# Normalised rows of the second routing made on ScalarE with a scale and a shift, instead of on GpSimd, in an attention and mixture-of-experts kernel

## The chip, the cores and the metric

The kernel runs on one core of a Trainium2 chip. Five engines work side by side, each through its own list of instructions in order: TensorE (PE in the profile, with its weight loads as PEld), VectorE (DVE), ScalarE (ACT), GpSimd (POOL) and SyncE (SP, which only issues transfers). An engine waits for another by semaphores. The metric is the device time of one execution in microseconds (us), lower is better.

## The reference

The input x has 8 batches of 256 tokens of 128 numbers, all float32. Three blocks follow each other, each adding to x:

```
x = x + 0.5 * ffn(layernorm(x))     # block f1
x = x + attn(layernorm(x))          # block at
x = x + 0.5 * ffn(layernorm(x))     # block f2
```

`layernorm(x)` is `(x - mean) / sqrt(var + 1e-5)` over the 128 numbers of a token. `ffn` is a mixture of 8 experts: a router (`xt @ Wr + br`) picks 2 experts for each token, each expert is two matrix products with a relu and a layernorm behind each, and the two results are weighed and added. `attn` is differential attention with 8 heads: two softmax maps for each head, one subtracted from the other, then a division by the root of the mean square of each head (rms) and an output projection.

## The kernel before

The order of the instructions is written out by hand; no planner is involved. The three blocks overlap. The middle of the program is a loop of *turns*, t = 2 to 9, in which each engine does pieces of four stages for four different batches:

- stage A, batch t (turns 2 to 7): layernorm, projections, packing of q and k;
- stage B, batch t-1 (to turn 8): scores for the row maxima (`scores(n)` on PE, six pieces; `row_max(b, n)` on DVE, line 2134);
- stage C, batch t-2: transposed scores (`scores_t(g)`, g = 0 to 7, on PE, lines 1900 to 1908), the exponential of each (`expo(g)` on ACT, line 1712), and products with the values (lines 1918 to 1922);
- stage D, batch t-3: combination of the maps (`outputs`, DVE line 2165), squares (`squares`, ACT line 1696), mean squares (DVE lines 2170 and 2171), the power -1/2 of them on POOL (line 1658, tile `orr`), its use on DVE (`rms`, line 2180), output projection, residual.

In turns 4 to 9 the *second routing*, for block f2, is worked in, for batch d = t-4: `row_stats` on DVE writes means and variances of the two tiles of 128 tokens into `mv`; `batch_norm(d)` on POOL (lines 1614 to 1623) makes the reciprocal deviation `rstd` (a power -1/2, line 1619) and then the normalised rows, one instruction of 128x128 for each tile (line 1622), into `rows_of` (the trace names it row_buf). Each of these adds 1 to the semaphore `F["xn"]` (f2_xn in the lists of order). Four things wait for it: `turn_batch(d)` on PE (line 627), which transposes the two tiles, `second_copies` on SP, which copies the rows once more beside themselves, the indirect transfers on POOL that scatter the rows to memory (line 459), and, for the last two batches, nothing of this change (`late_norm` on DVE makes their rows).

What matters is where these stand in the lists of the engines. ACT in a turn goes: expo(0), expo(1), copy of the transposed attention rows (line 917), `turned_batch` (line 620, copies the result of `turn_batch`), `squares`, expo(2), a copy of q (line 937), expo(3), and so on; in turn 9 `squares` stands between expo(0) and expo(1). PE goes: scores_t(0), scores(0), scores_t(1), transposes of the attention rows (line 1170, turns to 7), `turn_batch`, scores_t(2), scores(1), a projection (line 1176), scores_t(3), the router's products (`batch_logits`, lines 636 and 638), scores(2), and so on. While stage B runs, scores_t(g) may start only when expo(g-1) is done, since one pair of PSUM banks holds them, and scores(n) only when row_max(n-1) is done. POOL goes: power for the attention layernorm (line 559), `batch_norm`, then gathers or scatters of rows, `combine` (lines 1599 to 1605, turns to 6), and the power for the rms (line 1658).

Of the kernel before, what the change touches and what calls it, by code (L numbers as in the profile page):

```python
# [17 lines left out]
ALU = mybir.AluOpType  # L18
ACT = mybir.ActivationFunctionType
# [3 lines left out]
BATCH, SEQ, DIM = 8, 256, 128  # L23
# [26 lines left out]
HALF = TT // 2  # L50
# [58 lines left out]
def build(nc, x, Wq, Wk, Wv, Wo, lq1, lk1, lq2, lk2, Wr, br, W1, b1, g1, be1, W2, b2, g2, be2, out, stages=("f1", "at", "f2")):  # L109
    with ExitStack() as ctx:  # L110
        def sb(name, shape, dt=F32):
            return ctx.enter_context(nc.sbuf_tensor(name, shape, dt))
# [15 lines left out]
        xs = sb("xs", [P, TT, DIM])  # L128
        row_buf = [sb(f"row_buf{i}", [P, HALF * TOPK * ROW]) for i in range(2)]
        xn = row_buf[0][:, 0:TT * DIM].rearrange("p (t d) -> p t d", d=DIM)  # L130
# [25 lines left out]
        rows_of = [v[:].rearrange("p (t k w) -> p t k w", k=TOPK, w=ROW) for v in row_buf]  # L156
# [16 lines left out]
        mv = sb("mv", [P, TT, 2])  # L173
        sdev = sb("sdev", [P, TT])
        rstd = sb("rstd", [P, TT])
# [4 lines left out]
        m12 = sb("m12", [P, TOPK, TT])  # L180
# [1097 lines left out]

        def late_norm(dve, S, step, d):
            a, b = 2 * d, 2 * d + 2  # L1280
            dve.wait_ge(S["sd"], 2 * (BATCH - 2) + d - 5)
            step(dve.reciprocal(rstd[:, a:b], sdev[:, a:b]))
            for t in range(a, b):
                dve.tensor_scalar(rows_of[1][:, t % HALF, :, 0:DIM], xs[:, t, None, :].to_broadcast([P, TOPK, DIM]), mv[:, t, 0:1],
                                  rstd[:, t:t + 1], ALU.subtract, ALU.mult).then_inc(S["xn"], 1)
# [292 lines left out]
        def att_gpsimd(pool, S):  # L1578
# [33 lines left out]
            F = sems["f2"]  # L1612

            def batch_norm(d):
                a, b = 2 * d, 2 * d + 2
                pool.wait_ge(F["mv"], b)
                pool.tensor_scalar(sdev[:, a:b], mv[:, a:b, 1], EPS, None, ALU.add).then_inc(F["sd"], 1)
                pool.wait_ge(F["sd"], b - 1)
                pool.tensor_tensor(rstd[:, a:b], sdev[:, a:b], neg_half[:, 0:2], ALU.pow).then_inc(F["sd"], 1)
                pool.wait_ge(F["sd"], b)  # L1620
                for t in range(a, b):
                    pool.tensor_scalar(rows_of[t // HALF][:, t % HALF, 0, 0:DIM], xs[:, t, :], mv[:, t, 0:1], rstd[:, t:t + 1],
                                       ALU.subtract, ALU.mult).then_inc(F["xn"], 1)

            pool.wait_ge(S["yst0"], 8 * PAIRS)
            pool.wait_ge(S["yst1"], 8 * PAIRS)
# [50 lines left out]
        def att_scalar(act):  # L1677
# [7 lines left out]
            F = sems["f2"]  # L1685
            copy_xT, relu, copy_hT, sqrt1, sqrt2, finish = scalar_pair(act, F, False)

            def half_values(s, seq):

                act.wait_ge(A["o"], seq * 2 + s + 1)  # L1690
                act.copy(oTs[:, s].rearrange("p a e -> p (a e)"), bank[s][:]).then_inc(A["oTv"], 1)

            def squares(d):

                act.wait_ge(A["dstep"], d * D_STEPS + 3)
                act.activation(osq, od[:], ACT.Square).then_inc(A["dstep"], 1)
# [6 lines left out]
            def turn(t, par):  # L1703
                A_, B_, C_, D_ = stages_of(t)
                b, c, d = t - 1, t - 2, t - 3

                def expo(g):
                    act.wait_ge(A["st"], c * 8 + g + 1)
                    if not (isinstance(c, int) and c == 0):
                        act.wait_ge(A["o"], c * 2 - 1 + g // 4)  # L1710
                    low = 0 if B_ or g % 2 == 0 else 2
                    act.activation(prob[:, g], quad[:, low:low + 2, 0:3 * P], ACT.Exp).then_inc(A["prob"], 1)  # L1712
# [10 lines left out]
                if C_:  # L1723
                    expo(0)
                    if t == BATCH + 1:
                        squares(d)
                    expo(1)
                if A_:
                    turned_norm(act, t, bank[7])
                if 4 <= t <= BATCH + 1:  # L1730
# [32 lines left out]
            d = BATCH - 1  # L1763
# [618 lines left out]

        b1s = early[0:32, 5760:5760 + P]
        pads = sb("pads", [P, 8])
        hold, spad, gpad = pads[0:1, 0:2], pads[:, 2:3], pads[0:1, 4:6]


# [144 lines left out]
```

## Time and profile before

| what | value |
|---|---|
| time, median of 3 runs | 447.54 us (446.53 to 448.34) |
| span of the profiled execution, first to last instruction | 444.6 us |
| the profiled execution's own time | not recorded apart from its span |
| PE, DVE, ACT, POOL busy | 395.1, 348.4, 286.7, 246.8 us |
| turns 4 to 9 | about 207 to 320 us of the span |
| PE clock granted in the turns | full (1.00 in each stretch) |

The busy share says little about who holds up whom, since each engine's list is fixed and the turns run from one engine to another and back. A start time in a timeline, with the idle time and the releaser in brackets behind it, tells who was late. Times below are microseconds from the span's start.

### The profile page before, as it was taken

The page shows a single profiled execution, that of the slowest core. Times are in us where ns is not written, and L with a number is a line of the kernel's source. Part 1 is how long each engine was busy: PE and PEld are TensorE (multiplying, and loading weights), DVE is VectorE, ACT ScalarE, POOL GpSimd, SP SyncE. Part 2 cuts the span into 40 slices and gives each one's busy share as a digit, 9 for nine tenths or more (in the row PEclk, how much of TensorE's full clock was granted, in tenths as well). Part 3 has the DMA queues.
Part 4 walks back from the last instruction along what each step waited for, and adds up shares of the span by engine and source line. Part 5 has one row for each costly group of instructions (what it writes and reads, how often), then busy time and mean ns, then how long its engine had stood idle before and what let it go on. Part 6 is the DMA issues. An engine that isn't in the chain of part 4 may idle for free.

```text
span 444.6 us, 11683 instructions
## 1 busy us (share of the span) xinstructions
PE 395.1 (89%) x3605; PEld 278.5 (63%) x3606; DVE 348.4 (78%) x1302; ACT 286.7 (64%) x589; POOL 246.8 (56%) x348
## 2 busy tenths in 40 slices
PE   7989999999898857889888889976899899999984
PEld 7735487877676744556564656554577677878733
DVE  5886578887959886878897988976688968788865
ACT  1395687755676754787677777764765467667630
POOL 8685554436461136374847566576634758555540
PEclk9996999999999955999999999999999899999999
DMA  7920114554443411000000001001121221111127
GB/s 219 335 96 14 35 49 143 181 178 158 121 144 112 170 37 35 21 8 20 25 13 25 24 21 33 25 27 36 56 60 34 72 64 56 53 59 47 37 72 244
DMA packets 25862, 35.17 MB, mean 79 GB/s; under 512 B 4282, under 2 KB 18546, under 8 KB 24659
## 3 DMA queue, kind: packets, MB, share of 16 engines
q1 hardware_dynamic: 20866, 24.62, 16.7%
q0 software_dynamic: 4944, 9.90, 7.6%
q8 instruction: 28, 0.46, 0.4%
q14 instruction: 24, 0.19, 0.1%
HBM read 15.45 MB, written 18.24 MB: 76 GB/s over the span
## 4 chain that ended last, share of the span: by engine, by line
PE 51%; DVE 20%; issue 9%; POOL 8%; ACT 5%; DMA 3%; DVEq 1%; SPq 1%; POOLq 0%; ACTq 0%
PE bank L972 11%; PE bank L991 10%; PE bank L981 5%; DVE mx L2134 4%; POOL xr_scratch L459 3%; PE bank L1181 3%; PE bank L2495 2%; PE bank L1900 2%; DMA early<-y_scratch 2%; PE bank L1176 2%; ACT early L1712 1%; PE bank L1918 1%; POOL orr L1658 1%; PE bank L1852 1%; DMA y_scratch<-yo,dest_u 1%
## 5 line engine op out<-in xcount | busy, mean ns | idle before, releaser
L991 PEld LDWEIGHTS bank<-w2c,hT 128*128 128x128 f32 x624 | 76.5, 194 | 23.5 <-issue 22.6
L991 PE MATMUL bank<-w2c,hT 128*128 x624 | 78.1, 279 | 4.9 <-ACT hT L760 4.9
L972 PE MATMUL bank<-w1s,xT 128*128 x156 | 74.1, 596 | 0.7 <-DVE w2c L2369 0.6
L2134 DVE TENSOR_REDUCE mx<-bank 128x4 f32<-128x1024 f32 (+1 forms) x48 | 58.5, 1220 | 13.7 <-PE bank L1861 13.3
L1712 ACT ACTIVATE early<-bank 128x768 f32<-128x768 f32 x64 | 51.8, 812 | 23.7 <-PE bank L1908 23.0
L1377 DVE BATCH_NORM_STATS2 st<-wide 128x6 f32<-128x512 f32 x78 | 50.1, 683 | 19.8 <-ACT wide L754 19.7
L760 ACT COPY hT<-bank 128x1024 f32<-128x1024 f32 (+1 forms) x40 | 39.5, 988 | 34.0 <-PE bank L981 34.0
L513 POOL DMA_INDIRECT xgw<-xn_scratch,slot_u x39 | 37.4, 960 | 35.4 <-PE bank L961 24.3
L483 POOL DMA_INDIRECT y_scratch<-yo,dest_u x39 | 39.0, 1001 | 31.3 <-PE bank L981 16.8
L579 POOL DMA_INDIRECT yk<-y_scratch,posi x32 | 32.2, 1005 | 42.2 <-DMA y_scratch<-yo 17.4
L754 ACT ACTIVATE wide<-bank 128x1024 f32<-128x1024 f32 (+1 forms) x40 | 40.0, 1001 | 10.3 <-PE bank L972 9.6
L459 POOL DMA_INDIRECT xr_scratch<-row_buf,hi_i x32 | 31.8, 994 | 22.6 <-PE bank L1908 12.9
L981 PE MATMUL bank<-ident,wide 128*128 128x128 f32 x312 | 40.9, 274 | 1.3 <-issue 1.3
L972 PEld LDWEIGHTS bank<-w1s,xT 128*128 128x128 f32 x156 | 27.0, 190 | 22.0 <-issue 21.6
L981 PEld LDWEIGHTS bank<-ident,wide 128*128 128x128 f32 x312 | 35.3, 142 | 2.6 <-issue 2.0
L937 ACT COPY wide<-bank 128x1024 bf16<-128x1024 bf16 x28 | 28.4, 1014 | 5.7 <-PE bank L1181 5.6
L775 ACT ACTIVATE yo<-yz,r 128x128 f32<-128x128 f32 x78 | 27.1, 396 | 4.2 <-DVE yz L1420 2.6
L1396 DVE SCALAR_TENSOR_TENSOR yy<-bank,r,b2p 128x128 f32<-128x128 f32 x78 | 24.6, 351 | 6.1 <-DVE r L1390 1.6
L1900 PE MATMUL bank<-mxT,sel 64*128 64x384 bf16 x128 | 22.2, 343 | 7.2 <-ACT early L1712 5.1
L1852 PE MATMUL bank<-mrhs,mlhs 64*128 64x128 bf16 (+1 forms) x192 | 16.1, 248 | 11.4 <-DVE mx L2134 6.6
L1420 DVE SCALAR_TENSOR_TENSOR yz<-yy,mv,g2b 128x128 f32<-128x128 f32 x78 | 23.3, 339 | 0.0
L559 POOL TENSOR_TENSOR ars<-ave,neg_half 128x2 f32<-128x2 f32 x8 | 5.8, 720 | 31.2 <-DVE ave L2092 31.2
(380 smaller groups left out, 893.4 us busy)
## 6 DMA issues: line engine op xcount, KB each, us to landing
xr_scratch<-row_buf SPq DMA_DIRECT2D x8, 1032.0 KB
xgw<-xr_scratch SPq DMA_DIRECT2D x39, 64.5 KB, 1.8
y_scratch<-yo SPq DMA_DIRECT2D x19, 128.0 KB, 1.8
w1s<-in_L_ffn_W_dram SPq DMA_DIRECT2D x1, 2048.0 KB, 9.9
early<-y_scratch SPq DMA_DIRECT2D x8, 256.0 KB, 3.4
xn_scratch<-row_buf SPq DMA_DIRECT2D x1, 1024.0 KB
out_dram<-xs SPq DMA_DIRECT2D x8, 128.0 KB, 2.6
row_buf<-row_buf SPq DMA_DIRECT2D x6, 128.0 KB
```

The lines of the kernel that those rows point to most:

```text
L459: pool.indirect_dma_start(out=xr_dram, out_offset=bass.IndirectOffsetOnAxis(ap=slot2[:, c:c + 1], axis=0), in_=rows_of[t // HALF][:, t % H ...
L483: pool.indirect_dma_start(out=y_dram, out_offset=bass.IndirectOffsetOnAxis(ap=dest_u[:, 2 * p + j:2 * p + j + 1], axis=0), in_=yo[:, p % 2 ...
L513: pool.indirect_dma_start(out=xg[:, u, :], out_offset=None, in_=xn_dram, in_offset=bass.IndirectOffsetOnAxis(ap=slot_u[:, n:n + 1], axis=0 ...
L579: pool.indirect_dma_start(out=yk4[:, t % (2 * YRING), k, :], out_offset=None, in_=done, in_offset=bass.IndirectOffsetOnAxis(ap=posi[:, c:c ...
L754: act.activation(hh[:, u, 0:k, :], banks[:, h_at[u]:h_at[u] + k, :], ACT.Relu).then_inc(S["relu"], 1)
L760: act.copy(hT[:, u, 0:k, :], banks[:, 5:5 + k, :]).then_inc(S["hTc"], 1)
L972: last = pe.matmul(bank[h_at[u] + j][:], xT[:, u, j, :], w1s[:, bass.ds(e * FF, FF)], start=True, stop=True)
L981: last = pe.transpose(bank[5 + j][:, c * P:c * P + P], hh[:, u, j, c * P:(c + 1) * P], ident[:])
L991: last = pe.matmul(o[:, j * DIM:(j + 1) * DIM], hT[:, u, j, c * P:(c + 1) * P], w2c[:, bass.ds(e * (FC * DIM) + c * DIM, DIM)], start=(c = ...
L1377: last = dve.bn_stats(st1[:, u, j, :], hh[:, u, j, :])
L1712: act.activation(prob[:, g], quad[:, low:low + 2, 0:3 * P], ACT.Exp).then_inc(A["prob"], 1)
L2134: dve.tensor_reduce(mx[:, c:c + 2 * per].rearrange("p (a q) -> p q a", q=2), quad[:, low:low + 2, :].rearrange("p q (a e) -> p q a e", a=p ...
```

## The change

`batch_norm` on POOL no longer writes the rows. It makes four small tiles of 128x2 instead of two: the variance plus eps, minus the mean (new), the power -1/2, and the shift, minus mean times `rstd` (new). A new function `batch_rows(d)` on ACT then makes the two 128x128 tiles as `Identity(x * rstd + shift)`, with the scale and the shift read from tiles, one number for each partition. It stands in turns 4 to 9 right behind expo(1). Semaphore counts follow. The tiles `mean_at` and `shift_at` are parts of `m12`, which is free by then.

```diff
         def late_norm(dve, S, step, d):
             a, b = 2 * d, 2 * d + 2
-            dve.wait_ge(S["sd"], 2 * (BATCH - 2) + d - 5)
+            dve.wait_ge(S["sd"], 4 * (BATCH - 2) + d - 5)
...
                 pool.tensor_scalar(sdev[:, a:b], mv[:, a:b, 1], EPS, None, ALU.add).then_inc(F["sd"], 1)
-                pool.wait_ge(F["sd"], b - 1)
+                pool.tensor_scalar(mean_at[:], mv[:, a:b, 0], -1.0, None, ALU.mult).then_inc(F["sd"], 1)
+                pool.wait_ge(F["sd"], 4 * d + 2)
                 pool.tensor_tensor(rstd[:, a:b], sdev[:, a:b], neg_half[:, 0:2], ALU.pow).then_inc(F["sd"], 1)
-                pool.wait_ge(F["sd"], b)
-                for t in range(a, b):
-                    pool.tensor_scalar(rows_of[t // HALF][:, t % HALF, 0, 0:DIM], xs[:, t, :], mv[:, t, 0:1], rstd[:, t:t + 1],
-                                       ALU.subtract, ALU.mult).then_inc(F["xn"], 1)
+                pool.wait_ge(F["sd"], 4 * d + 3)
+                if d:
+                    pool.wait_ge(F["xn"], 2 * d)
+                pool.tensor_tensor(shift_at[:], mean_at[:], rstd[:, a:b], ALU.mult).then_inc(F["sd"], 1)
...
+            def batch_rows(d):
+
+                act.wait_ge(F["sd"], 4 * d + 4)
+                for t in range(2 * d, 2 * d + 2):
+                    act.activation(rows_of[t // HALF][:, t % HALF, 0, 0:DIM], xs[:, t, :], ACT.Identity, scale=rstd[:, t:t + 1],
+                                   bias=shift_at[:, t % 2:t % 2 + 1]).then_inc(F["xn"], 1)
+
...
                     expo(1)
+                if 4 <= t <= BATCH + 1:
+                    batch_rows(t - 4)
                 if A_:
                     turned_norm(act, t, bank[7])
...
+        mean_at, shift_at = m12[:, 0, 0:2], m12[:, 1, 0:2]
```

ACT in turn 7 (d = 3), from the second copy of k to expo(2), before:

```order
L937 COPY wide<-bank 128x8x128 [waits at_kTp]
L1712 ACTIVATE early<-bank 128x768 [waits at_o,at_st] x2
L917 COPY axT<-bank 128x256 [waits at_xTp]
L620 COPY xnT<-bank 128x256 [waits f2_lgp,f2_xnTp]
L1696 ACTIVATE turned_o<-od 128x256 [waits at_dstep]
L1712 ACTIVATE early<-bank 128x768 [waits at_o,at_st]
```

and the same place now (line numbers behind the new function are 8 higher; m is the tile m12):

```order
L937 COPY wide<-bank 128x8x128 [waits at_kTp]
L1720 ACTIVATE early<-bank 128x768 [waits at_o,at_st] x2
L1698 ACTIVATE row_buf<-xs,m,rstd 128x128 [waits f2_sd]
L1698 ACTIVATE row_buf<-xs,m,rstd 128x128
L917 COPY axT<-bank 128x256 [waits at_xTp]
L620 COPY xnT<-bank 128x256 [waits f2_lgp,f2_xnTp]
L1704 ACTIVATE turned_o<-od 128x256 [waits at_dstep]
L1720 ACTIVATE early<-bank 128x768 [waits at_o,at_st]
```

Two instructions stand new between expo(1) and the copies; nothing else of ACT's order moved.

POOL in turn 7, from the attention's power to the power for the rms, before:

```order
L559 TENSOR_TENSOR ars<-ave,neg_half 128x2 [waits at_var]
L1617 TENSOR_SCALAR sdev<-mv 128x2 [waits f2_mv]
L1619 TENSOR_TENSOR rstd<-sdev,neg_half 128x2 [waits f2_sd]
L1622 TENSOR_SCALAR row_buf<-xs,mv,rstd 128x128 [waits f2_sd]
L1622 TENSOR_SCALAR row_buf<-xs,mv,rstd 128x128
L459 DMA xr_scratch<-row_buf,hi_i 17280x129 [waits at_st,f2_xn,f2_pos]
L459 DMA xr_scratch<-row_buf,hi_i 17280x129 [waits f1_xnst,at_st]
L1658 TENSOR_TENSOR orr<-oms,neg_half 128x16 [waits at_msq]
```

and now:

```order
L559 TENSOR_TENSOR ars<-ave,neg_half 128x2 [waits at_var]
L1617 TENSOR_SCALAR sdev<-mv 128x2 [waits f2_mv]
L1618 TENSOR_SCALAR m<-mv 128x2
L1620 TENSOR_TENSOR rstd<-sdev,neg_half 128x2 [waits f2_sd]
L1624 TENSOR_TENSOR m<-m,rstd 128x2 [waits f2_xn,f2_sd]
L459 DMA xr_scratch<-row_buf,hi_i 17280x129 [waits at_st,f2_xn,f2_pos]
L459 DMA xr_scratch<-row_buf,hi_i 17280x129 [waits f1_xnst,at_st]
L1659 TENSOR_TENSOR orr<-oms,neg_half 128x16 [waits at_msq]
```

Two large instructions are gone and two small ones are there. The order of PE, DVE and SP is the same as before.

## Rows read from the trace of the kernel before

**Rows 1.** Waits, 185 to 330 us: who waited for whom, total, times, longest (us).

```profile
PEld bank L1900 <- ACT early L1712: 11.7, 24, 1.5
```

**Rows 2.** Instructions by line, POOL, 190 to 330 us: busy us, mean ns.

```profile
L1622 POOL TENSOR_SCALAR row_buf<-xs,mv,rstd 128x128 f32<-128x128 f32 x12 | 10.1, 842 | 0.7
L1617 POOL TENSOR_SCALAR sdev<-mv 128x2 f32<-128x2 f32 x6 | 1.5, 242 | 2.9 <-DVE mv L1190 2.8
```

**Rows 3.** Instructions by line and form, ACT, whole span.

```profile
L775 ACT ACTIVATE yo<-yz,r 128x128 f32<-128x128 f32 x78 | 27.1, 396 | 4.2 <-DVE yz L1420 2.6 <-DMA y_scratch<-yo,dest_u 1.4
L768 ACT ACTIVATE sd<-mv,eps_c 128x2 f32<-128x2 f32 x38 | 11.0, 289 | 6.7 <-DVE mv L1408 6.6
L923 ACT COPY vnew<-bank 128x128 f32<-128x128 f32 x16 | 4.4, 274 | 0.0
L812 ACT ACTIVATE pads<-eps_c 128x1 f32<-128x1 f32 x1 | 0.2, 203 | 0.0
```

**Rows 4.** Timeline of ACT, 333 to 339 us: start, length, instruction.

```profile
335.52 0.68 ACT L775 ACTIVATE yo<-yz,r 128x128 f32<-128x128 f32 x2
```

**Rows 5.** Timelines of turn 7 (268.8 to 288.1 us): ACT, PE, DVE.

```profile
273.76 0.81 ACT L1712 ACTIVATE early<-bank 128x768 f32<-128x768 f32 x1 [0.71 <-PE bank L1908]
...
274.72 0.39 ACT L620 COPY xnT<-bank 128x256 f32<-128x256 f32 x1
...
275.30 0.82 ACT L1712 ACTIVATE early<-bank 128x768 f32<-128x768 f32 x1
...
274.19 0.41 PE L627 MATMUL bank<-ident,row_buf 128*128 128x128 f32 x2
274.63 0.34 PE L1900 MATMUL bank<-mxT,sel 64*128 64x384 bf16 x2
...
278.22 1.23 DVE L2134 TENSOR_REDUCE mx<-bank 128x4 f32<-128x1024 f32 x1 [0.20 <-PE bank L1861]
```

**Rows 6.** Timelines of turn 8 (288.1 to 306 us): PE, DVE.

```profile
293.49 0.42 DVE L2165 TENSOR_TENSOR od<-ow 128x256 f32<-128x256 f32 x1
...
293.93 0.34 PE L1900 MATMUL bank<-mxT,sel 64*128 64x384 bf16 x2 [0.54 <-ACT early L1712]
...
294.93 0.17 DVE L2171 TENSOR_SCALAR oms<-oms 128x16 f32<-128x16 f32 x1
```

**Rows 7.** Timeline of turn 4 (207.4 to 228.0 us), all engines.

```profile
212.25 0.81 ACT L1712 ACTIVATE early<-bank 128x768 f32<-128x768 f32 x1 [0.71 <-PE bank L1908]
...
212.68 2.07 DVE L2165 TENSOR_TENSOR od<-ow 128x256 f32<-128x256 f32 x1
...
215.69 0.76 DVE L2171 TENSOR_SCALAR oms<-oms 128x16 f32<-128x16 f32 x1
...
216.36 1.21 DVE L2134 TENSOR_REDUCE mx<-bank 128x8 f32<-128x1024 f32 x1
```

**Rows 8.** Timeline of turn 5 (228.0 to 248.7 us), all engines.

```profile
237.63 2.94 POOL L1658 TENSOR_TENSOR orr<-oms,neg_half 128x16 f32<-128x16 f32 x1
...
240.60 0.42 DVE L2180 TENSOR_TENSOR od<-od,orr 128x256 f32<-128x256 f32 x1 [1.44 <-POOL orr L1658]
```

**Rows 9.** Timelines of turn 6 (248.7 to 268.8 us): DVE, ACT.

```profile
253.68 0.81 ACT L1712 ACTIVATE early<-bank 128x768 f32<-128x768 f32 x1 [0.71 <-PE bank L1908]
...
254.11 1.30 DVE L2165 TENSOR_TENSOR od<-ow 128x256 f32<-128x256 f32 x1
...
255.76 0.79 ACT L1712 ACTIVATE early<-bank 128x768 f32<-128x768 f32 x1
...
258.93 1.22 DVE L2134 TENSOR_REDUCE mx<-bank 128x4 f32<-128x1024 f32 x1 [0.54 <-PE bank L1861]
```

**Rows 10.** Timeline of turn 9 (306 to 320 us), all engines.

```profile
311.12 0.80 ACT L1712 ACTIVATE early<-bank 128x768 f32<-128x768 f32 x1
...
311.38 0.41 PE L627 MATMUL bank<-ident,row_buf 128*128 128x128 f32 x2 [0.87 <-POOL row_buf L1622]
...
316.84 0.42 DVE L2180 TENSOR_TENSOR od<-od,orr 128x256 f32<-128x256 f32 x1 [1.36 <-POOL orr L1658]
```

## The prediction, on record before the changed kernel ran

> **What bounds the kernel now.** I read the table of waits of the attention turns first, then the timelines of turns 4 to 9 engine by engine, then the instructions by line for prices. The change touches nothing outside these turns, so only they count. What the reader should see: TensorE and ScalarE pass the turn to and fro. the transposed scores waited 11.7 us in 24 places for the exponential before them [rows 1], and each exponential needs its scores. That is one loop, scores_t(g), expo(g), scores_t(g+1), and time put into it between expo(1) and scores_t(2) is not hidden by either engine's idle time. In turns 7 and 8 nothing else is late at that place: scores_t(2) starts at 274.63, 0.06 behind the end of expo(1) at 274.57 [rows 5], and at 293.93 with "<-ACT early" as its releaser [rows 6]. The transposes of the normalised rows (line 627) lie at 274.19, beside expo(1), where they cost nothing, because GpSimd had the rows ready before.
>
> GpSimd is the other candidate. In turn 5 VectorE waits 1.44 us for its power of the mean squares (tile orr), in turn 9 1.36 us, and in turn 9 TensorE waits 0.87 us for the rows themselves [rows 8, 10]. So a lighter GpSimd is worth something in two or three turns, and nothing in the others.
>
> **What is removed.** Twelve GpSimd instructions of 0.84 us, two in each of six turns [rows 2]. Added on GpSimd are two of 128x2 in each turn. Minus the mean is of the kind of line 1617, 0.24 us. The shift is a product of two 128x2 tiles, which the trace does not show at that size; I take the same 0.24, since the instruction is of the same size, with 0.1 for the semaphore between. So GpSimd is free 1.68 - 0.58 = 1.1 us earlier in each turn. Bounds: 1.68 if the small ones cost nothing, 0 if each took as long as a removed one. It finishes the shift well ahead of expo(1)'s end, so ScalarE does not wait for it: in turn 9, where it is latest, TensorE got the rows at 311.38 [rows 10], the shift would be there at about 310.2, and expo(1) ends at 311.92.
>
> **What is added on ScalarE.** Two instructions of 128x128 with scale and bias both read from tiles. The trace has none of these. The nearest is line 775, one operand from a tile, 0.396 us, and 0.68 for a pair [rows 3, 4]. A bias read from a tile costs 0.289 - 0.203 = 0.086 (line 768 against 812); the same step shows between line 923, 0.274, and line 775. So one takes about 0.48. The pair, with the overlap of 2 x 0.396 - 0.68 = 0.11 that line 775 shows, takes 0.85, and since it overlaps expo(1)'s end as well, it ends 0.75 behind it. Bounds: 0.34 (two like line 923, with both overlaps) and 0.96 (two of 0.48 end to end). The Trainium skill ("ScalarE: Activation LUTs", section "What ACT_TABLE_LOAD costs") gives 186 ns plus 0.833 ns for each element, 93 ns more for each pointer operand, and an overlap of 93; that makes 0.48 and 0.87 for the pair, beside line 775's 0.396 against the page's 0.386.
>
> **What it costs on the path.** `turn_batch` now waits for ScalarE, and behind it on TensorE stands scores_t(2). Behind expo(1)'s end come: 0.75 for the rows, 0.07 for the semaphore, 0.44 for the transposes (274.19 to 274.63 [rows 5]). scores_t(2) thus starts 1.26 behind expo(1) instead of 0.06: 1.2 us later. ScalarE's side is longer still: it waits for these transposes before its copy (line 620), and copy and squares take 0.58 (274.72 to 275.30 [rows 5]), so expo(2) cannot start before 2.0 us behind expo(1)'s end. What was 0.1 to 0.5 us of slack becomes the chain. Turn by turn:
>
> - Turn 7: expo(2) goes from 275.30 to 276.5, the products behind it and row_max(2) with them; row_max(2) waited for TensorE before (278.22 [rows 5]), so nothing absorbs it. +1.2.
> - Turn 8: the same loop, scores_t(2) at 293.93 [rows 6]. +1.2.
> - Turn 6: expo(1) ends at 254.49, expo(2) started 1.27 behind it, at 255.76, because DVE's `outputs` took 1.30 us where it took 0.42 in turn 8 [rows 6, 9]. It moves to 256.5, +0.7; row_max(2) at 258.93 is then held by TensorE's order about 0.5 later. +0.5.
> - Turn 4: `outputs` took 2.07 us, so squares and expo(2) were late anyway, and ScalarE's new path ends at 213.06 + 2.0 = 215.1, where expo(2) stood (212.68 + 2.07, then the squares). Then the small line 2171 took 0.76 at 215.69, against 0.17 in turn 8 [rows 6, 7]; this ought to shrink, since GpSimd will be past its adds. row_max(1) at 216.36 comes about 0.6 earlier. -0.6.
> - Turn 5: the +1.2 arrives at VectorE's `rms` at 240.4; the power, which started at 237.63 behind GpSimd's queue, starts 1.1 earlier at 236.5 and ends at 239.5. Before, `rms` was at 240.60 [rows 8]. -0.2.
> - Turn 9: expo(1) ends at 311.92, the transposes move from 311.38 to 312.75, the row of exponentials behind by 1.4. But `rms` waited for the power until 316.84 [rows 10] and TensorE behind it; that comes 1.1 earlier. What is left at the output projection is +0.3.
>
> Sum: 1.2 + 1.2 + 0.5 - 0.6 - 0.2 + 0.3 = +2.4 us. The span of 444.6 becomes 447.0. The runs' median lies 2.9 us above the span, which holds what is ahead of the first and behind the last instruction; I leave that as it is: 447.5 + 2.4 = 449.9.
>
> The contention in turns 4 and 6 is weighed once more, as it speaks for the change: `outputs` reads two SBUF tiles and took 2.07 and 1.30 us where GpSimd worked at the same time. The Trainium skill ("GPSIMD Engine Reference", "Specifications") says that GpSimd shares its SBUF interfaces with VectorE and contends with instructions of two SBUF inputs; the trace agrees with it by those two rows. By that the gain is in how GpSimd's work shifts against VectorE's, and 1.1 us of shift can take a hold away in one turn and make one in another (in turn 5, `outputs` starts where GpSimd's product then would). Both stand off ScalarE's new path of 2.0 us as long as the hold is under 1.5 us.
>
> **Rivals.** (a) *No measurable change.* The turns have more slack than I see: the delay of scores_t(2) is absorbed in row_max's own queue on VectorE, and only turns 7 and 8 pay, less the gains in 4, 5 and 9 (-0.6, -0.2, 0): 2.4 - 0.8 = +1.6; with the pair at its low bound, 0.34, the two turns pay 0.4 less each, +0.8. For it: VectorE is busy through most of a turn. Against it: in turn 7 row_max(2) still waited 0.20 for TensorE. Time 448.3 to 449.1. (b) *Faster.* GpSimd is the real bound: the two waits for the power (1.44, 1.36) and the wait for the rows (0.87) [rows 8, 10] go, 3.7 us at most, and turn 4's hold goes too (2.07 - 0.45 = 1.6). Turns 7 and 8 still pay 2.4, so 2.4 - 5.3 = -2.9, 444.6; it decides if the new step of 1.2 is hidden in turns 5, 6 and 9 altogether. Against it: ScalarE's chain of 2.0 us stands in all six turns. (c) *Every turn pays in full*: 6 x 1.2 = 7.2 us, 454.7, if the earlier GpSimd makes new holds on VectorE where it lifted old ones. (d) *Reload of ScalarE's table* for Identity between two exponentials would cost some 1.3 us twice in each turn, over 15 us; the order of the changed kernel has the same five loads as before, none in the turns, so I give it next to nothing.
>
> **How the numbers follow.** The forecast (+1.8 to +4) has 0.5, rival (a) 0.3 (+0.5 to +1.8), (b) 0.1 (below that), (c) and (d) 0.1. About 0.5%, 2.2 us, is what a measurement of this kernel can tell from no change, and the forecast lies just above that. Slower by over 0.5% (above 449.8): a little over half of the forecast's cases and all of (c), 0.47. Faster by over 0.5% (below 445.3): most of (b), 0.06. Within: 0.47. The range leaves out a part of (b) and of (c): 447.3 to 452.4. The forecast's own range is 449.3 to 451.5.
>
> **What would show it.** Right: line 1698 twice in each turn, 0.45 to 0.5 us each; the transposes at line 627 with ScalarE's rows as releaser in turns 5 to 9; scores_t(2) 1.2 to 1.3 behind expo(1)'s end; expo(2) 2.0 behind it; turns 7 and 8 1.2 us longer; orr about 1 us earlier against its turn in turns 5 and 9, and not the releaser of `rms` in turn 5. Wrong: turns 7 and 8 as long as before (19.3 and 17.9 us, by the stretches that head rows 5 and 6), or `rms` in turns 4 to 6 so early that the turns get shorter, or `outputs` held over 1.5 us in turns that had no hold.

## The result, and the profile after

| | before | after |
|---|---|---|
| time, median of 4 runs each | 447.24 us (446.53 to 448.34) | 456.54 us (456.28 to 457.72) |
| ratio, 95% interval | | 1.0195 [1.0153, 1.0237] |
| span of the profiled execution | 444.6 us | 455.8 us (its run: 457.72) |
| mean granted clock of TensorE | 0.965 | 0.949 |

Slower by 9.3 us (1.95%, clear of the noise), where +2.4 was forecast; the time lies 4 us above the range. First the page of the changed kernel: span, busy times, and the clock that TensorE was granted in 40 slices.

```profile
span 455.8 us, 11700 instructions
PE 401.2 (88%) x3605; PEld 281.2 (62%) x3606; DVE 347.8 (76%) x1302; ACT 291.8 (64%) x601; POOL 239.2 (52%) x348
PEclk9898999999999967999799999979799999999997
```

and the same line of the page of the kernel before:

```profile
PEclk9996999999999955999999999999999899999999
```

ScalarE got 5.1 us more work and GpSimd 7.6 less, as expected. But PE is busy 6.1 us longer with the same 3605 instructions, and its clock line shows a 7 in slices 20, 27 and 29 (of 11.4 us each, from 216.5, 296.2 and 319.0 us on), where the line of before has a 9 in all of them. (The low digits in slices 15 and 16 stand in both lines, ahead of the turns in question; the last slice, with a 7 for a 9, is behind them.) So there are two things to look for: the loop that the prediction spoke of, and TensorE's clock.

**The loop.** The waits from 185 to 340 us after (who waited for whom, total, times, longest), against [rows 1]:

```profile
ACT early L1720 <- PE bank L1918: 22.7, 27, 3.5
...
PE bank L627 <- ACT row_buf L1698: 9.6, 6, 2.3
DVE oms L2180 <- ACT turned_o L1704: 9.1, 7, 2.0
PEld bank L1910 <- ACT early L1720: 8.9, 19, 1.1
```

and the new instruction of ScalarE (ns min/median/max, first and last start):

```profile
L1698 ACT ACTIVATE row_buf<-xs,m,rstd x12: 482/482/491, 212.3 to 319.1; 128x128 f32<-128x128 f32 x12
```

In all six turns TensorE now waits for ScalarE's rows, which never happened before. Turn 7 of the changed kernel, PE and ACT, against [rows 5]:

```profile
275.88 0.81 ACT L1720 ACTIVATE early<-bank 128x768 f32<-128x768 f32 x1 [0.71 <-PE bank L1918]
276.59 0.87 ACT L1698 ACTIVATE row_buf<-xs,m,rstd 128x128 f32<-128x128 f32 x2
...
278.05 0.37 ACT L620 COPY xnT<-bank 128x256 f32<-128x256 f32 x1 [0.33 <-PE bank L627]
278.31 0.42 ACT L1704 ACTIVATE turned_o<-od 128x256 f32<-128x256 f32 x1
278.63 0.80 ACT L1720 ACTIVATE early<-bank 128x768 f32<-128x768 f32 x1
...
277.60 0.41 PE L627 MATMUL bank<-ident,row_buf 128*128 128x128 f32 x2 [1.39 <-ACT row_buf L1698]
277.94 0.34 PE L1910 MATMUL bank<-mxT,sel 64*128 64x384 bf16 x2
```

expo(1) ends at 276.69, scores_t(2) starts at 277.94, 1.25 behind it (forecast 1.26), and expo(2) at 278.63, 1.94 behind (forecast 2.0). The mechanism is there to the tenth.

**The clock.** I measure a turn from the first transposes of the row maxima (line 1931 before, 1941 after) to the next; turn 9 to the start of the step on VectorE that makes hi_i, the rows' places, for its batch (L699 after, the sixth of the second routing). In us:

| kernel | turn 4 | 5 | 6 | 7 | 8 | 9 to hi_i |
|---|---|---|---|---|---|---|
| before | 20.75 | 20.68 | 20.08 | 19.30 | 18.68 | 10.51 |
| changed | 23.30 | 20.52 | 20.49 | 20.48 | 22.27 | 12.18 |
| difference | +2.55 | -0.16 | +0.41 | +1.18 | +3.59 | +1.67 |
| forecast | -0.6 | -0.2 | +0.5 | +1.2 | +1.2 | +0.3 |

Turns 5, 6 and 7 came out within 0.1 of the forecast. Turns 4, 8 and 9 are 3.2, 2.4 and 1.4 longer than it, and these three hold the slices with a 7 in the clock line. Two stretches of turn 4, turn 8's and turn 9's in the changed kernel (length; busy us and instructions of PE, PEld, DVE, ACT, POOL; PEclk; DMA share, GB/s):

```profile
208.39:214.39 6.00, 4.09 (x67) 2.73 (x66) 4.22 (x7) 4.59 (x10) 5.11 (x12) 1.00 0.04 11
214.39:224.39 10.00, 10.00 (x111) 5.77 (x107) 6.14 (x15) 5.56 (x12) 4.55 (x3) 0.66 0.08 21
...
293.18:299.18 6.00, 3.72 (x65) 2.53 (x64) 2.84 (x5) 4.33 (x9) 3.31 (x5) 1.00 0.08 25
299.18:309.18 10.00, 8.84 (x115) 5.55 (x113) 5.95 (x13) 4.63 (x8) 5.01 (x3) 0.66 0.07 20
...
315.45:319.73 4.28, 1.39 (x26) 0.87 (x23) 3.09 (x12) 3.06 (x6) 2.77 (x5) 1.00 0.10 31
319.73:327.63 7.90, 7.90 (x78) 4.54 (x78) 4.40 (x27) 3.62 (x5) 3.35 (x2) 0.57 0.24 62
```

Each turn begins at 2.4 GHz (1.00); in the stretch that follows the wait for the rows most of the time is at 1.2 GHz, which I call half clock (from about 214.5 to 222, 300 to 307 and 320.5 to 327.5). The same products take up to 1.7 times as long there. Turn 8, PE:

```profile
298.08 0.41 PE L627 MATMUL bank<-ident,row_buf 128*128 128x128 f32 x2 [1.76 <-ACT row_buf L1698]
...
300.95 1.02 PE L638 MATMUL bank<-wrs,xnT 128*128 128x8 f32 x4
...
304.05 0.39 PE L1862 MATMUL bank<-mrhs,mlhs 64*128 64x128 bf16 x4 [0.47 <-DVE mx L2144]
...
304.80 1.08 PE L1928 MATMUL bank<-early,vaug 128*32 128x256 f32 x8
```

At full clock L638 takes 0.61 and L1928 0.64, as the runs below show. The rest of the +11.2 of the span: -0.7 ahead of turn 4, +1.4 from the sixth hi_i to the seventh, +1.2 in what follows, where either trace has half clock once more (352 to 356 before, 450 to the end after).

### The profile page after: what moved, and what is told of

Its sections match the earlier page's. It is cut to its first block, busy times and chain, and to the rows that moved or that the text cites. A ratio compares the mean times of both kernels' runs of the same rounds, so it can differ in the third digit from the quotient of the medians.

```text
span 455.8 us, 11700 instructions
## 1 busy us (share of the span) xinstructions
PE 401.2 (88%) x3605; PEld 281.2 (62%) x3606; DVE 347.8 (76%) x1302; ACT 291.8 (64%) x601; POOL 239.2 (52%) x348
## 4 chain that ended last, share of the span: by engine, by line
PE 54%; DVE 15%; issue 10%; ACT 8%; POOL 6%; DMA 5%; DVEq 1%; SPq 1%; POOLq 0%; ACTq 0%
PE bank L972 10%; PE bank L991 9%; PE bank L981 5%; DVE mx L2144 3%; PE bank L1181 3%; PE bank L1176 3%; ACT early L1720 3%; PE bank L1910 3%; POOL xr_scratch L459 2%; PE bank L1928 2%; DMA early<-y_scratch 2%; PE bank L1862 2%; PE bank L2361 1%; PE bank L1930 1%; PE bank L2011 1%
## 5 line engine op out<-in xcount | busy, mean ns | idle before, releaser
L991 PEld LDWEIGHTS bank<-w2c,hT 128*128 128x128 f32 x624 | 75.2, 192 | 24.3 <-issue 23.5
L991 PE MATMUL bank<-w2c,hT 128*128 x624 | 76.8, 276 | 5.7 <-ACT hT L760 5.7
L1659 POOL TENSOR_TENSOR orr<-oms,neg_half 128x16 f32<-128x16 f32 x7 | 20.5, 2932 | 5.2 <-DVE oms L2181 3.7
## 6 DMA issues: line engine op xcount, KB each, us to landing
w1s<-in_L_ffn_W_dram SPq DMA_DIRECT2D x1, 2048.0 KB, 10.9
```

The source lines that it names most:

```text
L991: last = pe.matmul(o[:, j * DIM:(j + 1) * DIM], hT[:, u, j, c * P:(c + 1) * P], w2c[:, bass.ds(e * (FC * DIM) + c * DIM, DIM)], start=(c = ...
```

## Experiments

All ratios are to runs of the kernel before on the same chip; edits are against the changed kernel. The median of the kernel before differs between these sets of runs, 447.15 to 448.32 us, so times of two experiments can be compared to about 1 us, and ratios are the better measure. A clock or a turn length is that of one traced execution. The turn lengths of all runs are in a table at the end of this section.

**rows_before_expo1**: the rows ahead of expo(1).

```diff
+                    if t in (4, 5, 6, 7, 8, 9):
+                        batch_rows(t - 4)
                     expo(1)
-                if 4 <= t <= BATCH + 1:
-                    batch_rows(t - 4)
```

> The changed kernel with the two row instructions on ScalarE between expo(0) and expo(1) (in turn 9 behind the squares) instead of behind expo(1). There ScalarE waited 0.71 us for TensorE before expo(1), the shift is ready (209.97 + 0.28 = 210.25 in turn 4, expo(0) ends at 210.86), and the rows are ready 0.8 us behind expo(0), before TensorE comes to the transposes. Theory 'wait on TensorE' (the loss is TensorE's wait for the rows and what follows from it): the wait of 1.39 to 2.32 us before line 627 goes, and with it the three stretches of half clock; GpSimd's 1.1 us stay saved: 445 to 447.5 us, against 456.5 for the change. Rival 'ScalarE's time' (0.87 us more in each turn on an engine in the loop is the loss wherever it stands): expo(1) and all behind it comes 0.8 later in each turn: 452 us or more.

446.21 us, ratio 0.9951 [0.9928, 0.9975]: half a per cent faster than the kernel before, and 10.3 us faster than the changed one. Its turn 7 (ACT and PE):

```profile
270.53 0.88 ACT L1698 ACTIVATE row_buf<-xs,m,rstd 128x128 f32<-128x128 f32 x2
271.34 0.81 ACT L1720 ACTIVATE early<-bank 128x768 f32<-128x768 f32 x1
...
271.56 0.41 PE L627 MATMUL bank<-ident,row_buf 128*128 128x128 f32 x2
272.20 0.34 PE L1910 MATMUL bank<-mxT,sel 64*128 64x384 bf16 x2 [0.24 <-ACT early L1720]
```

expo(1) waited 0.71 for its scores in turns 4 to 8; the pair takes up that idle time, and the transposes lie beside expo(1) again. Turns 7 and 8 are back at 19.29 and 18.67. So the place of the pair, not its work, costs the 1.2 us. The gain over before is in turns 4, 5, 6 and 9 (-0.75, -0.16, -0.79, -0.53: 2.2 together, which is the ratio's), where GpSimd was late. In this trace no turn runs at half clock.

**transpose_later**: rows behind expo(1) as in the change, but TensorE's transposes one step later, behind scores_t(2), and their copy behind expo(2).

```diff
-                    if t >= 4 and g == 1:
+                    if t >= 4 and g == 2:
                         pe.wait_ge(A["ow"], t - 2)
                         turn_batch(pe, F, t - 4)
```

> The changed kernel with the transposes of the rows on TensorE moved behind scores_t(2) and scores(1), and ScalarE's copy of them moved behind expo(2). The rows stay behind expo(1). Theory 'wait on TensorE': the rows are ready when TensorE comes to them, scores_t(2) starts 0.1 us behind expo(1) again, no stretch of half clock in turns 4, 8 and 9; what stays is ScalarE's 0.77 us before expo(2), where there was 0.1 to 0.5 of slack: 447 to 449.5 us. Rival 'ScalarE's time': nearly all of the loss stays, 454 or more.

449.06, 1.0032 [1.0006, 1.0058]. Turns 6 to 8 cost 0.2 more than with early rows, not 1.2, and of the six waits only turn 9's is left, 1.24 us; half clock follows it (312 to 319), and turn 9 takes 11.75. So it is the order of TensorE's list, with scores_t(2) queued behind the rows' transposes, that makes the loop longer. The time is as expected, the full clock in turn 9 is not.

**gpsimd_busy_again**: rows early, and GpSimd does its twelve removed instructions all the same, into a tile nobody reads.

```diff
+                for t in range(a, b):
+                    pool.tensor_scalar(gsT[:], xs[:, t, :], mv[:, t, 0:1], rstd[:, t:t + 1], ALU.subtract, ALU.mult).then_inc(s_idle, 1)
```

> The rows between expo(0) and expo(1) on ScalarE, and GpSimd gets its two instructions of 128x128 back, writing to a tile that nobody reads. It leaves nothing out of the computation. Theory 'GpSimd's time' (that kernel gains on the one before because GpSimd is 1.1 us earlier): turns 4, 5 and 6 go back from 20.0, 20.5, 19.3 us to at least the 20.75, 20.7, 20.1 of before, and the time to 447.5 to 449.5, equal to the kernel before or a little above it. Rival 'ScalarE has the rows sooner' (rows made sooner than on GpSimd are the gain): stays at 446.2.

450.53, 1.0058 [1.0027, 1.0090], against 0.9951 without that work. Turns 4, 5, 6 and 9 get 1.05, 0.74, 0.60 and 0.96 longer, turns 7 and 8 0.2 and 0. This is 1 us more than I expected and slower than the kernel before, for GpSimd carries more here than it did there, the twelve and the new small ones as well: VectorE waits for its power in turns 4, 5, 6, 7 and 9 (1.44, 1.44, 0.84, 0.45 and 1.69 us), where before it did in turns 5 and 9. So GpSimd's time is worth what rows_before_expo1 gains, and the rival is out, but this run does not bring the kernel before back turn by turn. Half clock from 313.5 to 317.5 has a part in turn 9.

**late_only_in_5_to_7**, **late_only_in_4**, **late_only_in_8**: rows early, but behind expo(1) in the turns named.

```diff
+                    if t in (4, 5, 6, 7, 9):
+                        batch_rows(t - 4)
                     expo(1)
-                if 4 <= t <= BATCH + 1:
+                if t in (8,):
                     batch_rows(t - 4)
```

> The rows behind expo(1), as in the change, only in turns 5, 6 and 7, whose clock stayed at 1.00; between expo(0) and expo(1) in turns 4, 8 and 9. Theory 'clock': these three turns cost what their lengths show (20.5, 20.5, 20.5 us against 20.7, 20.1, 19.3: +1.4 together) and the others gain a little: 446.5 to 449 us, no new stretch of half clock. Rival 'delay only': each turn pays its sixth of 9.3 us, so 451 to 452 us.

449.78, 1.0049 [1.0022, 1.0075]. The time lies between the two ranges, 0.8 above the clock theory's. Turns 6 and 7 are 1.20 longer than with early rows, turn 5 not at all: there `outputs` on VectorE takes 1.85 us in both kernels, beside GpSimd's work, and holds expo(2) back either way. Turn 9 has half clock here (315 to 318), against the expectation.

> The rows behind expo(1) in turn 4 alone, between expo(0) and expo(1) in turns 5 to 9. TensorE waits 1.39 us for the rows in turn 4, as in the change. Theory 'clock': the wait and the clock's fall behind it make turn 4 22 to 23.3 us long against 20.0 with the rows early everywhere, so 2 to 3.3 us more than the 446.2 of that kernel: 448 to 449.5. Rival 'delay only': 1.2 us more, 447.4, and no half clock.

448.5, 1.0016 [0.9986, 1.0046]. Turn 4 takes 20.37, 0.37 more than early, with the full wait of 1.39 us, and the clock stays:

```profile
208.50:214.50 6.00, 4.09 (x65) 2.73 (x64) 4.23 (x7) 4.48 (x10) 5.11 (x12) 1.00 0.04 11
214.50:224.50 10.00, 9.66 (x154) 6.07 (x148) 8.61 (x23) 8.24 (x16) 5.75 (x5) 1.00 0.10 28
```

Compare turn 4 of the changed kernel above: the first six microseconds are the same to the hundredth (PE busy 4.09 of 6.00), the ten behind them are at 0.66 there and at 1.00 here. So this wait makes a fall possible and does not decide it. That the time came out as expected is luck: turn 4 did not fall, and turn 9, which has early rows here, did (11.67 for 9.98, half clock from 311 to 317.5).

> ScalarE's rows stand behind expo(1) in turn 8 alone, ahead of it in the five other turns; all is computed. Theory (the wait of 1.4 us adds 1.2 us to turn 8, and TensorE's fall to 1.2 GHz the rest of that turn's 3.6): if the wait alone is followed by the fall, turn 8 takes 21.4 to 22.3 us and the time is 448.5 to 449.5; if the fall needs what came before in the other late turns, turn 8 takes 19.9 without half clock, and the time is 447.3 to 448. Rival (turn 8 is long by a wait of the loop, whatever the clock): 21.4 or more with full clock.

453.0, 1.0137 [1.0078, 1.0196], 3.5 us more than I had given it even with the fall. One late turn alone costs 6.8 us against all rows early (8.3 by the ratios), where all six cost 10.3 (10.9):

```profile
288.67:294.67 6.00, 3.72 (x65) 2.52 (x64) 2.84 (x5) 4.33 (x9) 3.33 (x5) 1.00 0.07 22
294.67:304.67 10.00, 9.08 (x105) 5.53 (x101) 5.03 (x12) 4.03 (x7) 4.26 (x3) 0.51 0.07 21
```

Turn 8 takes 23.36, where early rows give 18.67, and turn 9, with rows early, 11.46 in place of 9.98, with half clock from 315 to 322.5. My numbers counted the first and left out the second.

**fill_wait** and **fill_whole_wait**: unneeded transposes of 128x128 (identity by identity, into a bank that is free there) while TensorE waits for the rows. 5 in each of the six turns, then 11, 14 and 18 (turns 4 to 7, 8, 9).

```diff
         def turn_batch(pe, S, d):
+            for _ in range({4: 14, 5: 18}.get(d, 11) if d < BATCH - 2 else 0):
+                pe.transpose(routing_banks(d)[0][:, 0:P], ident[:], ident[:])
```

> The changed kernel with five transposes of the identity into the bank that the row transposes write next, on TensorE just ahead of its wait for the rows, in turns 4 to 9. They add work of about 1.1 us to a wait of 1.39 to 2.32 us and change no wait. Theory 'clock' (6 to 7 of the 9.3 us are TensorE at half its clock after waits of over 1.3 us at this place in turns 4, 8 and 9; the rest is the delay of 1.2 us in the loop): the granted clock stays 1.00 in turns 4, 8 and 9, and the time comes down to 449 to 451 us. Rival 'delay only' (the time is lost in the waits themselves, and the lower clock slows nothing that counts): 456.5 or more, whatever the clock shows.

451.49, 1.0092 [1.0060, 1.0125]. One filler took some 0.11 us, so five covered less than half of a wait (0.75 of 1.39 us are left, 0.97 of 1.76 in turn 8, 1.53 of 2.32 in turn 9). The time is 0.5 above the clock theory's range, and its clock of 1.00 did not come: turn 4 does not fall in this trace (20.31), turns 8 and 9 do.

> The changed kernel with fillers that cover the whole wait: 11 transposes of the identity in turns 4 to 7, 14 in turn 8, 18 in turn 9. In the run with five in each turn they took 0.49 us for three, so five covered about half of the wait; the fall in turn 4 was gone (20.31 us against 23.30 for the turn), those behind turns 8 and 9 were shorter but there. Theory 'clock': with the whole wait covered no stretch of half clock follows it in turns 4, 8 and 9; turn 8 comes to 18.67 + 1.2 = 19.9 us and the time to 448.5 to 450.5 us, so that the delay in the loop alone is left. Rival 'turns 8 and 9 lose by something else' (their own order of work): turn 8 stays at 21.4 or more and the time at 451.5 or more.

452.46, 1.0106 [1.0057, 1.0155], a miss: 2 us above what I expected. Turn 9 is mended (9.98), turn 8 is not (21.45; half clock from 300.5 to 304.5). Ahead of that fall a second wait shows, 0.81 us for the row maximum that scores(3) needs; in fill_wait, too, the fall in turn 8 (302 to 305.5) comes 0.7 us behind this wait and 5.7 behind the one for the rows. But the wait by itself is nothing new. It stands in the kernel before (first line) and is the same in this run (second line):

```profile
298.49 0.29 PE L1852 MATMUL bank<-mrhs,mlhs 64*128 64x128 bf16 x4 [0.81 <-DVE mx L2134]
```

```profile
300.34 0.29 PE L1864 MATMUL bank<-mrhs,mlhs 64*128 64x128 bf16 x4 [0.81 <-DVE mx L2146]
```

The six kernels whose rows are early in turn 8 have it as well (0.80 or 0.81 us), and turn 8 keeps its clock in all seven traces.

**fill_turn8_both**: the same, and 8 fillers in that second wait.

```diff
+                        if t == BATCH and g == 4:
+                            for _ in range(8):
+                                pe.transpose(bank[0][:, 0:P], ident[:], ident[:])
                         scores(g - 1)
```

> As the changed kernel, with 11 to 18 unneeded transposes of 128x128 ahead of the rows' transposes in turns 4 to 9, as in fill_whole_wait, and 8 more ahead of scores(3) of turn 8, where TensorE waited 0.81 us for row_max(2); all is computed. Clock theory: no half clock in turn 8, which takes about 19.9 us in place of 21.45, and 450 to 451 in all. Rival (the fall in turn 8 isn't from these two waits): turn 8 stays at 21.3 to 21.6 with half clock in it, 452 to 453 in all.

450.98, 1.0068 [1.0033, 1.0103]; no half clock in the turns, turn 8 19.97, as the clock theory said. The rival is out. The changed kernel, run again beside it (change_again, below), took 456.81, so the fillers are worth 5.8 us here.

**fill_turns8_9_only**: fillers in turns 8 (14 and 8) and 9 (18) alone.

> As fill_turn8_both, but without the unneeded transposes in turns 4 to 7 (TensorE waits 1.4 us there again): 14 and 18 ahead of the rows' transposes of turns 8 and 9, 8 ahead of scores(3) of turn 8; all is computed. Clock theory with the falls bound to turns 8 and 9: turns 4 to 7 take 20.3 to 20.5 us as they are, turn 8 19.9 to 20.0, and the time is that of fill_turn8_both, 450 to 451.5 (turn 4 may fall by chance, as in one of two traces of the change: then turn 4 23.3 and 453 to 454). Rival (the turns before wear the clock down, and turn 8 falls for their waits): turn 8 21.4 to 23.4 with half clock, 453 to 455.

449.65, 1.0045 [1.0016, 1.0073]: the changed kernel with all its six late rows and its work, 6.9 us faster by 40 products that do nothing (6.7 by the ratios). Turn 8, the two fillings and the value products:

```profile
294.05 1.75 PE L625 MATMUL bank<-ident 128*128 128x128 f32 x14
295.78 0.44 PE L629 MATMUL bank<-ident,row_buf 128*128 128x128 f32 x2
...
298.36 0.61 PE L640 MATMUL bank<-wrs,xnT 128*128 128x8 f32 x4
...
299.86 1.09 PE L1966 MATMUL bank<-ident 128*128 128x128 f32 x8
...
301.32 0.64 PE L1930 MATMUL bank<-early,vaug 128*32 128x256 f32 x8
```

Turns 4 to 7 wait 1.39 us each as in the change and keep their clock, and turn 8 keeps its own behind them; in late_only_in_8 it fell without them. So the waits of turns 4 to 7 are neither enough for turn 8's fall nor needed for it.

**fill_mx_wait_only**: the 8 fillers of the second wait alone.

> As the changed kernel, with 8 unneeded transposes ahead of scores(3) of turn 8 and no others; all is computed. If the wait of 1.76 us for the rows alone is followed by the fall, turn 8 takes 21.4 to 23.4 us with half clock, and the time is 454 to 457. If the fall needs the second wait too, turn 8 takes 19.9 to 20.1 at full clock, and the time is 452 to 454.

458.29, 1.0257 [1.0202, 1.0311], turn 8 22.91 with half clock from 297 to 304. The time is 1.3 us above the range. The wait for the rows alone is followed by the fall. With late rows, then, turn 8 fell when either wait was left open (three traces here: fill_wait, fill_whole_wait and this one) and kept its clock in the two in which both were filled. The second wait is not enough by itself, since turn 8 of the kernel before has it at full clock; what late rows add to it once their own wait is filled is not shown.

**turn9_rows_first** (rows in all turns ahead of expo(1), in turn 9 ahead of `squares` too) and **rows_early_fill9** (rows early, 14 fillers in turn 9) try to better the early version.

```diff
                     expo(0)
+                    if 4 <= t <= BATCH + 1:
+                        batch_rows(t - 4)
                     if t == BATCH + 1:
                         squares(d)
                     expo(1)
```

> As the kernel with the rows between expo(0) and expo(1), but in turn 9 the rows stand ahead of the squares. There the transposes waited 1.62 us for the rows, at 309.70, and the power for the rms started at 310.81 behind GpSimd's scatter, 1.8 us behind the squares. Moving the rows ahead brings them 0.3 us forward and the squares 0.8 us back, still ahead of the scatter's end. Theory: transposes and all exponentials behind them 0.3 earlier, the power the same: 0 to 0.3 us less, within the noise of 446.2. Rival: the squares become late for the power: 0.5 more.

446.72, 0.9973 [0.9947, 1.0].

> ScalarE's rows ahead of expo(1) in all six turns, and 14 unneeded transposes ahead of the rows' transposes in turn 9 alone, where TensorE waited 1.62 us; all is computed. The wait in turn 9 was followed by no half clock with the rows early, so if the clock there is safe, the fillers give nothing: 446 to 446.8. If the time from turn 9 on gains by a steadier clock, 445 to 446. If the fillers run past the rows' arrival, 446.5 to 447.5.

447.2, 0.9988 [0.9953, 1.0022], 0.4 above the range for fillers that give nothing. Neither is better than rows_before_expo1 (in the medians; the intervals overlap), and turn 9 takes 9.97 or 9.98 with all three. That rows_before_expo1 kept its clock in turn 9 is not a property of the kernel: the four other kernels with the same wait of 1.62 there (the three late_only ones and gpsimd_busy_again) show half clock in it. The windows on both sides of the end of that wait (columns as above), for rows_before_expo1 and then for late_only_in_8, are nearly alike ahead of it and differ in the clock behind it (in late_only_in_8 the fall begins 0.3 us ahead of the wait's end, and turn 8 before it had fallen too; in late_only_in_4 and late_only_in_5_to_7 turn 8 had not, and turn 9 fell all the same):

```profile
306.10:309.70 3.60, 1.41 (x26) 0.89 (x24) 2.50 (x8) 2.51 (x6) 2.21 (x4) 1.00 0.06 18
309.70:316.09 6.39, 6.34 (x92) 4.07 (x94) 4.94 (x32) 4.87 (x8) 3.91 (x2) 1.00 0.19 54
```

```profile
312.03:315.61 3.58, 1.39 (x25) 0.88 (x23) 2.49 (x8) 2.50 (x6) 2.20 (x4) 0.96 0.06 18
315.61:323.49 7.88, 7.88 (x78) 4.76 (x80) 5.00 (x32) 4.19 (x7) 3.90 (x2) 0.59 0.22 61
```

**change_again**: the changed kernel once more, for a second trace.

> The changed kernel once more, for a second trace of it. If the falls of TensorE's clock belong to the kernel's own timing, they stand again in turns 4, 8 and 9, which take 23.3, 22.3 and 12.2 us (to hi_i(5)), and the time is 456 to 457. If they are chance, turns 4 and 8 show 20.3 and 19.9 to 21.5 in this trace and the profiled execution takes 451 to 454.

456.81, 1.0203 [1.0144, 1.0261]. Turns 8 and 9 fall again (23.35 and 12.13), turn 4 does not (20.36), with the same wait of 1.39:

```profile
209.04:215.04 6.00, 4.09 (x67) 2.73 (x66) 4.22 (x7) 4.59 (x10) 5.12 (x12) 1.00 0.04 11
215.04:225.04 10.00, 9.66 (x150) 5.91 (x146) 8.79 (x24) 8.06 (x16) 5.56 (x4) 1.00 0.10 28
```

Turn 4 fell only in the first trace, then, and turns 8 and 9 in both. This pair prices the clock without any edit: the same kernel, the same wait, and turn 4 takes 23.30 us with the fall and 20.36 without. The span is 1.0 us shorter in all: 2.9 less in turn 4, against 1.1 more in turn 8, whose half clock was longer (297.5 to 308 for 300 to 307), 0.7 more ahead of turn 4 and 0.2 in the rest.

Turn lengths (us) of all runs; a star marks half clock inside:

| kernel | 4 | 5 | 6 | 7 | 8 | 9 to hi_i |
|---|---|---|---|---|---|---|
| change_again | 20.36 | 20.52 | 20.48 | 20.50 | 23.35* | 12.13* |
| rows_before_expo1 | 20.00 | 20.52 | 19.29 | 19.29 | 18.67 | 9.98 |
| transpose_later | 19.98 | 20.50 | 19.50 | 19.49 | 18.92 | 11.75* |
| gpsimd_busy_again | 21.05 | 21.26 | 19.89 | 19.49 | 18.68 | 10.94* |
| late_only_in_5_to_7 | 19.97 | 20.52 | 20.49 | 20.49 | 18.67 | 10.14* |
| late_only_in_4 | 20.37 | 20.51 | 19.30 | 19.29 | 18.67 | 11.67* |
| late_only_in_8 | 19.97 | 20.52 | 19.29 | 19.29 | 23.36* | 11.46* |
| fill_wait | 20.31 | 20.51 | 20.43 | 20.42 | 21.45* | 10.74* |
| fill_whole_wait | 20.30 | 20.52 | 20.42 | 20.43 | 21.45* | 9.98 |
| fill_turn8_both | 20.31 | 20.52 | 20.43 | 20.42 | 19.97 | 9.96 |
| fill_turns8_9_only | 20.37 | 20.53 | 20.48 | 20.49 | 19.97 | 9.97 |
| fill_mx_wait_only | 20.37 | 20.52 | 20.49 | 20.48 | 22.91* | 12.30* |
| turn9_rows_first | 19.97 | 20.51 | 19.30 | 19.29 | 18.67 | 9.97 |
| rows_early_fill9 | 19.97 | 20.51 | 19.29 | 19.29 | 18.66 | 9.97 |

## Why the prediction was wrong

The step that failed is one the prediction took without writing it down: that every product keeps its length, since the clock was full in all stretches of the turns before. Every term of the sum moved a wait and none asked what TensorE's clock would do when TensorE has 1.4 to 2.3 us of new idle time in each turn. With that time filled in turns 8 and 9 the same kernel takes 449.65 us, 0.25 from the 449.9 that was forecast; without, 456.5. So of the 9.3 us some 2 to 3.5 are the loop's and what follows from it, and 6 to 7 the clock's (5.8 by fill_turn8_both, 6.9 by fill_turns8_9_only).

By its own steps:

- *The pair of rows, 0.85, from 0.48 each.* 0.482 and 0.87. Right.
- *GpSimd 1.1 us earlier, small instructions 0.24.* By the lines of the changed kernel, POOL, 190 to 330 us (busy, mean ns), against [rows 2]:

```profile
L1617 POOL TENSOR_SCALAR sdev<-mv 128x2 f32<-128x2 f32 x6 | 1.5, 249 | 3.2 <-DVE mv L1190 2.8
L1618 POOL TENSOR_SCALAR m<-mv 128x2 f32<-128x2 f32 x6 | 1.3, 224 | 0.5
L1624 POOL TENSOR_TENSOR m<-m,rstd 128x2 f32<-128x2 f32 x6 | 1.3, 209 | 0.5
```

  Right in the sizes: 0.43 added for 1.68 removed in a turn. But the power for the rms started only 0.6 us earlier against its turn in turn 5 (7.24 us behind the turn's start for 7.82) and 0.5 in turn 9 (4.69 for 5.23), half of the 1.1, since in turn 5 it then waited for line 2181 and in turn 9 it still stood behind GpSimd's scatters of the rows. VectorE no longer waits for orr anywhere in the turns; the waits of 1.44 and 1.36 us [rows 8, 10] are gone.
- *scores_t(2) 1.26 behind expo(1), expo(2) 2.0.* 1.25 and 1.94. Right.
- *Turns 7 and 6: +1.2, +0.5.* +1.18 and +0.41. Right. In turn 6 the 1.2 us of the new order were set against 0.8 of relief, as rows_before_expo1 shows (19.29 against 20.08).
- *Turn 5: -0.2.* -0.16, as the forecast had it, but with the hold that the prediction named as a sign of being wrong: `outputs` took 1.84 us in place of 0.48, over its bound of 1.5. It still ended early enough, at 237.15, and expo(2) started at 237.63, 1.94 behind expo(1)'s end, as in the turns without a hold. The bound was too low; the time came out by the path, not by this reckoning.
- *Turn 4: -0.6.* By the mechanism -0.4 (20.36 in change_again); the expected easing of the holds is there, `outputs` 1.29 for 2.07 and line 2181 0.17 for 0.76 [rows 7]. In the first trace the fall of the clock put 2.9 on top.
- *Turn 8: +1.2.* +1.29 with full clock (fill_turns8_9_only). With the clock +3.6 and +4.7.
- *Turn 9: +0.3.* -0.53 with full clock: early rows and filled late rows give the same 9.97, so the new wait of 2.3 us is hidden there altogether, and what GpSimd gives comes through. With the clock +1.7. Mis-sized, with the wrong sign.

The mechanism's own turns sum to -0.4 - 0.15 + 0.4 + 1.2 + 1.3 - 0.5 = +1.8, a little under 2.4; that the filled kernel's median comes within 0.25 us of the forecast is in part luck, for its trace also has 0.7 us more between the sixth and the seventh hi_i and 1.0 more behind it than the kernel before, and the prediction had nothing there. The 2.9 us between span and time was misread too: in the traced execution of the change 1.9 us lie between its own time and its span, and the other 1.0 is the distance of a traced execution from the median. Rival (b) had its gains right in place (GpSimd's lateness was worth 2.2 us, not 5.3) but not its condition, that the new step is hidden. Rival (c), 454.7, came nearest to the time, for another reason: its turns 5 and 6 would have been 1.2 longer. No rival had the clock in it, and the range had no room for one. No reload of ScalarE's table: the rows start at 276.59, beside the end of expo(1), and the copy behind them starts at once; the traces of both kernels have five loads of 1.28 us, none of them between 163 and 320 us.

The numbers at hand said enough to ask. TensorE had been idle at this place for 0.1 us in turn 7, and the prediction itself worked out 1.2 us of new idle time. And the clock line of the kernel before has a 5 in slices 15 and 16: from 158 to 178 us, where TensorE was busy 14.2 of 20.4 us, it ran at half clock. "The clock is full in each stretch" was read as a property of the turns, where with more idle time in them it no longer held.

Still open: why turns 5 to 7 never fell, in five traces with a wait of 1.39 us in each of them (the two of the change, late_only_in_5_to_7, fill_turns8_9_only, fill_mx_wait_only), and turn 4 in one of five (the two of the change, late_only_in_4, fill_turns8_9_only, fill_mx_wait_only). In turn 8 TensorE has less to do ahead of the wait (3.72 of its first 6 us busy against 4.09 in turns 4 and 7; there is no attention layernorm and no projection in that turn) and waits longer, 1.76. That fits, but I did not test it apart. When a fall comes is open too: turn 8's half clock began 1.2 to 2.0 us behind the end of the wait for the rows in the four traces with 1.76 us of it, turn 9's from 0.4 us ahead of that end to 2.0 behind it. Open as well is the stretch between the sixth and the seventh hi_i, with no change in it: 16.35 before, 16.64 with early rows, 16.9 to 17.8 in all others, turn9_rows_first among them, where no turn fell.

## What to carry to other kernels

Count new idle time of TensorE twice: once as a delay, and once as a chance that its clock is halved for the next several microseconds. Here the granted clock had been 1.00 throughout these turns, and the second came to two to three times the first. A helper instruction on a neighbouring engine belongs where that engine already waits (here 0.71 us ahead of expo(1)), not between the instruction that releases TensorE and TensorE's next product. And to price the clock by itself, fill the waits with products that nobody reads, no more of them than the wait holds: what comes back is its share.

## What the runs showed of the hardware that was not expected

- Around waits of 1.2 to 2.3 us TensorE's granted clock fell from 2.4 to 1.2 GHz for some 3.5 to 10 us (314 to 317 in gpsimd_busy_again, 300 to 307 in the change, 297.5 to 308 in change_again), though TensorE was busy 3.72 of the first 6 us of turn 8, the wait among them. That turn fell in all four traces in which its 1.76 us were left unfilled (the two of the change, late_only_in_8, fill_mx_wait_only). It also fell in fill_wait and fill_whole_wait, 0.7 and 0.5 us behind the wait of 0.81 for the row maximum, a wait that seven traces with rows early or on GpSimd have at full clock. Turn 9 fell in 9 of the 11 traces in which 1.24 to 2.32 us were left.
- The same kernel with the same wait fell in turn 4 in one trace and not in the next, with PE busy 4.09 of the turn's first 6.00 us, the wait among them, in both. So a trace with a full clock does not show that the place is safe.
- Products that do nothing sped a kernel up by 6.9 us (456.5 to 449.65), 1.5%; in another set of runs by 5.8 (456.81 to 450.98). An fp32 transpose of 128x128 between two identities took 0.125 us in a row of fourteen.
- A ScalarE activation of 128x128 with both scale and bias from tiles took 0.482 us (0.482 to 0.491 in twelve). By the figures of the Trainium skill ("ScalarE: Activation LUTs", section "What ACT_TABLE_LOAD costs"), 186 ns, 0.833 ns for each element and 93 ns for each pointer operand, the estimate is 0.479; the trace agrees.
